# Who rounds the prepared weight sums in stage 2: ScalarE or VectorE

## The reference

```
h = relu(layernorm(x))
h_neigh = segment_sum(h[src], dst)
h = h @ Ws1 + h_neigh @ Wn1 + b1
h_neigh = segment_sum(h[src], dst)
out = x + h @ Ws2 + h_neigh @ Wn2 + b2
```

## Time and profile before

| what | value |
|---|---|
| median of three runs | 656.73 us |
| the profiled execution | 655.63 us |
| its span | 653.8 us |
| TensorE busy | 640.9 us (98%) |
| GpSimd busy | 210.3 us (32%) |
| VectorE busy | 286.0 us (44%) |
| ScalarE busy | 174.3 us (27%) |

### The profile page before, as it was taken

The page is one execution under the profiler, slowest core; times in us unless marked ns, Lnnn a source line. Parts: engine busy times, 40 slices in busy tenths (PEclk is TensorE's granted clock), DMA queues, the critical chain, the costliest instruction groups (busy, mean ns, idle before and its releaser), DMA issues.

```text
span 653.8 us, 8550 instructions
## 1 busy us (share of the span) xinstructions
PE 640.9 (98%) x3304; PEld 556.3 (85%) x3304; DVE 286.0 (44%) x392; ACT 174.3 (27%) x292; POOL 210.3 (32%) x198
## 2 busy tenths in 40 slices
PE   7999989999999999999999999999999999999997
PEld 5788778887899989999999988888888888887885
DVE  6763898871112111210022483325387987611111
ACT  5454243222123222313233122211334333100000
POOL 6224352000256666576580158003214012000000
PEclk9999999999999999999999999999999999999999
DMA  8622321003165676466754686444322242011111
GB/s 299 213 53 43 94 90 49 33 34 128 57 216 201 209 237 246 143 227 239 257 224 163 230 259 218 154 145 155 126 82 81 72 157 95 32 65 49 61 48 63
DMA packets 62726, 90.63 MB, mean 139 GB/s; under 512 B 16546, under 2 KB 34988, under 8 KB 62679
## 3 DMA queue, kind: packets, MB, share of 16 engines
q1 hardware_dynamic: 42342, 76.08, 34.6%
q10 hardware_dynamic: 20336, 13.91, 6.8%
HBM read 58.49 MB, written 31.48 MB: 138 GB/s over the span
## 4 chain that ended last, share of the span: by engine, by line
PE 62%; DMA 1%; DVE 0%; issue 0%; ACT 0%; POOL 0%; SPq 0%; DVEq 0%
PE PS L1274 29%; PE PS L1290 14%; PE PS L1237 10%; PE PS L1245 9%; DMA quarters<-ws_in 1%; DVE W_st L1021 0%; POOL prep_sum L624 0%; ACT W_st L750 0%; DVE s L1089 0%; ACT prep L801 0%; SPq L493 0%; DVEq L1088 0%
## 5 line engine op out<-in xcount | busy, mean ns | idle before, releaser
L1274 PE MATMUL PS<-right,left 128*128 128x512 f32 x840 | 190.6, 389 | 0.0
L1274 PEld LDWEIGHTS PS<-right,left 128*128 128x128 f32 x840 | 157.7, 188 | 32.7
L1109 PE MATMUL PS<-W,HT 128*128 128x512 f32 (+1 forms) x456 | 114.7, 399 | 2.7 <-ACT y_out L674 1.8
L1237 PE MATMUL PS<-HT,W_st 128*128 128x416 f32 (+1 forms) x576 | 110.7, 352 | 2.4 <-DVE W_st L1021 1.4
L1237 PEld LDWEIGHTS PS<-HT,W_st 128*128 128x128 f32 x576 | 107.9, 188 | 4.4 <-issue 3.4
L1109 PEld LDWEIGHTS PS<-W,HT 128*128 128x128 f32 (+1 forms) x456 | 81.3, 185 | 21.3 <-ACT y_out L674 2.9
L1245 PE MATMUL PS<-AT,y_st 128*128 128x416 f32 (+2 forms) x480 | 92.2, 351 | 0.0
L1245 PEld LDWEIGHTS PS<-AT,y_st 128*128 128x128 f32 (+1 forms) x480 | 90.1, 188 | 0.8
L657 POOL TENSOR_TENSOR left_sum<-h1T 128x640 f32<-128x640 f32 x24 | 41.9, 1747 | 150.2 <-PE PS L1274 119.9
L624 POOL TENSOR_TENSOR prep_sum<-quarters 128x512 f32<-128x512 f32 x40 | 52.7, 1320 | 100.0 <-PE PS L1109 62.8
L1290 PE MATMUL PS<-y_high,AT 128*128 128x512 f32 (+1 forms) x200 | 78.3, 392 | 0.0
(11 more groups left out here) (96 smaller groups left out, 476.9 us busy)
## 6 DMA issues: line engine op xcount, KB each, us to landing
sums_dram<-prep SPq DMA_DIRECT2D x40, 512.0 KB, 2.9
right<-sums_dram SPq DMA_DIRECT2D x40, 512.0 KB, 3.5
y_dram<-y_out ACTq DMA_DIRECT2D x18, 256.0 KB, 2.0
y_st_raw<-y_dram ACTq DMA_DIRECT2D x8, 576.0 KB
s<-x_in SPq DMA_DIRECT2D x18, 256.0 KB
out<-s SPq DMA_DIRECT2D x18, 256.0 KB
xin<-x_in SPq DMA_DIRECT2D x8, 512.0 KB, 11.6
W_raw<-wn_in SPq DMA_DIRECT2D x16, 256.0 KB, 5.1
```

The lines of the kernel that those rows point to most:

```text
L1109: ins = nc.tensor.matmul(PS[:r, bank, :], HT[:, a, k, t * P:t * P + r], W[:, k, b, :], start=first and m == 0, stop=last and m == 2)
L1237: ins = nc.tensor.matmul(PS[:, banks[c], 0:w_], W_st[:, a, k, :], HT[:, b, k, o_:o_ + w_], start=k == 0 and m == 0, stop=False)
L1274: ins = nc.tensor.matmul(PS[:, BANKS2[g % 8], :], left[:, k, a, i * P:(i + 1) * P], right[:, KB - 1 - k, b, :], start=k == 0 and j == 0, s ...
```

## The change

`prepare_high` moves from ScalarE's program to VectorE's, as a `tensor_copy` (a cast) in place of an activation with Copy. VectorE takes part 2j behind the LO part of `W_st` of tile j, and part 2j+1 behind the LO part of `y_st` of tile j. Part 1 is now behind tile 0's `y_st`, part 2 behind tile 1's `W_st`, and part 13 behind tile 6's `y_st`.

```diff
@@ ScalarE @@
-            def prepare_high(part):
-                for i in prepared(part):
-                    act.wait_ge(prep_summed, i + 1)
-                    nc.scalar.activation(prep[:, i % PREP, HI, :], prep_sum[:, i % PREP, LO, :], ACT.Copy).then_inc(prep_hi, 1)
-
             for j in range(KF - 1):
                 load_w_st(j + 1)
-                prepare_high(2 * j + 1)
                 w_st_high(j + 1)
                 load_y_st(j + 1)
                 h1_save(j, j % 2)
                 y_st_high(j + 1)
-                prepare_high(2 * j + 2)
@@ VectorE @@
+            def prepare_high(part):
+                for i in prepared(part):
+                    dve.wait_ge(prep_summed, i + 1)
+                    nc.vector.tensor_copy(prep[:, i % PREP, HI, :], prep_sum[:, i % PREP, LO, :]).then_inc(prep_hi, 1)
+
             for j in range(KF):
                 dve.wait_ge(wst_hi, j + 1)
                 nc.vector.tensor_tensor(W_st[:, LO, :, :], W_st_raw[:, LO, :, :], W_st[:, HI, :, :].bitcast(F32),
                                         ALU.subtract).then_inc(wst_lo, 1)
+                prepare_high(2 * j)
                 dve.wait_ge(yst_hi, 2 * j + 2)
...
+                prepare_high(2 * j + 1)
```

## The result

| | median us | range us | runs |
|---|---|---|---|
| before | 655.16 | 652.37 to 659.24 | 22 |
| changed | 652.43 | 650.46 to 656.15 | 21 |

The ratio is 0.9956 with a 95% interval of 0.994 to 0.9972: 1.8 to 3.9 us faster, 2.7 by the medians. The profiled execution of the changed kernel took 654.48 us, its span is 652.7.

What follows compares the result with a forecast made beforehand. TensorE, busy 98% of the span, was taken as the bound. Stall -1.5, casts 0 and `y_st` 0.1 made -1.4, so 654.2 us; with the runs' median 1.1 higher, 655.3, taken as 655.1. Range 653.8 to 657.5.

Steps and rivals of the forecast that it cites:

- the likeliest case: Whole kernel: the stage 2 stall goes and the casts hide behind TensorE; 655.1 us, own range 653.9 to 655.9, chance 0.57.
- The sum: Whole kernel: -1.5 for the stall, 0 for casts, 0.1 for `y_st`, so -1.4; 654.2 us, then taken as 655.1.
- the anchor: Whole kernel: the runs' median lies 1.1 us above the profiled execution's 655.63, which lifts 654.2 to 655.3; 655.1 taken.
- the gain: Stage 2: removing TensorE's 1.4 us wait, with slow first matmuls behind it, saves 1.5 us.
- The third rival: Runs' spread: all of it came from the wait for `W_st`, giving 653.9 us; held within the forecast's lower end, no separate chance.
- The removed part: ScalarE in stage 2: without high parts in its order, `W_st`'s high part starts when its load lands; the 1.4 us stall goes.
- The load of W: Stage 2, third tile: `W_st`'s load, issued at 230.03, lands after 4.5 us, leaving a margin of 3.4 to 4.4 us.
- The cast and its port: VectorE: 40 casts take turns with GpSimd on whole instructions, 0.28 us of turn each, bounds 0.28 and 1.46.
- GpSimd's batch: GpSimd: five sums, five low parts, the wait for quarters and shared turns take 19.6 to 22.0 us, typically 20.8; limit 21.9.
- the 2.6 us head start: First high part: VectorE is free at 178.1 where ScalarE began at 180.71, so sum 5 begins at about 191.
- The limit's place, cast 30: VectorE, ahead of tile 5's `y_st` low part: cast 30 must be done by about 303.3; second rival, 660.5 us, chance 0.14.
- `y_st`: Stage 2: its low part's margin thins from 1.5 to 0.2 us; costed at 0, bound 0.5 in each of three tiles.

Runs made afterwards that it cites:

- the odd parts alone: Against the kernel before, only the odd parts' high-part casts go to VectorE, the even parts stay on ScalarE behind `y_st`'s high part: ratio 0.999 (0.9965 to 1.0016).

## Why the prediction was wrong

The measured 652.46 us lies under the range of 653.8 to 657.5. The direction and the stall that goes were those of the likeliest case; the size was not.

- **The sum.** This is the step that failed, in two terms. First the anchor, the larger: I added 1.1 to the profiled execution's 655.63 to come to the median of three runs, 656.73. Over 22 runs the median is 655.16, so the term is -0.5; that is 1.6 of the 2.6 us between 655.1 and 652.46. Without it the sum gave 654.2, and I set that aside. Second the gain: I forecast 1.6 and held that even a perfect change takes no more than 1.4 to 1.7 us out of stage 2. The timed runs gave 2.7, at least 1.8. The profiles gave 1.6, the size I forecast but not made as I said: the waits are 0.8 of it, in place of 1.4, and the matmuls' step, which I did not see in the rows, is in the rest. Where the other 1.1 us of the timed gain come from stays open. The third rival, 653.9, came nearest by its number, not by its reason: it laid all of the runs' spread to this wait, and the changed kernel's runs still spread over 5.7 us, where those of before spread over 6.9.
- **Slips of sums.** 656.7 - 3 is 653.7 and not 653.9, 656.7 + 4 is 660.7 and not 660.5, and 1.4 us over 655.1 is 656.5 and not 656.2. None of them brings the measured time into the range.
- **The removed part.** The stall went, 26.58 to 25.04 us, though not from every execution (0.7 and 0.4 us in two of six profiles). But the reason I gave, that ScalarE's queue is cleared, is only one of two that suffice. In the changed kernel the same sum stands ahead of W on VectorE. It does no harm since it comes 4.7 us sooner, and the odd parts alone, which clear ScalarE's queue, gain nothing (0.999). I had both facts, the queue and the 2.6 us head start, and used the second only for the deadlines.
- **The load of W.** Costed at 4.5 us to landing, margin 3.4 to 4.4; it was 6.3 in the third tile, margin 2.3. The sooner quarters now go out just ahead of W's load there, a meeting that I had looked for at `y_st` only.
- **The cast and its port.** Right in kind: whole instructions take turns. 0.41 us alone, 1.5 beside GpSimd; it costs GpSimd 0.18, less than the 0.28 taken. The Trainium skill (SBUF — State Buffer, Who interferes with whom) says that the one that comes second fully blocks, and the trace agrees: 1.49 us for a cast of 0.41.
- **GpSimd's batch.** Predicted 20.8 us; from the loads of quarters at 185.55 and, six batches on, at 311.09 it is 20.9. Part of this is luck, as two errors cancel: the ten operations with all turns took 14.9 where I had 15.5, the wait for quarters 5.8 where I had 5.3. Sum 39 was to begin near 327 and began at 327.7. The limit's place, cast 30, is where TensorE did wait with two more casts each; that GpSimd is the bound there was not borne out (21.5 us a batch, and 21.9 wanted).
- **`y_st`.** No wait of TensorE, as forecast. The second tile's low parts ended at 199.67 for 205.2; its load, at 191.75, no longer ran right behind quarters, which had gone out at 185.55. In one of the six profiles of the changed kernel the weights waited 0.4 us for it.

## What to carry to other kernels

A wait for slow work from another stage costs by what stands behind it in the engine's order, so there are two cures: put the urgent work ahead, or make the slow work come sooner. They don't add up; joined without care they were 1% slower, since putting the urgent work ahead also held back what releases the next slow load. And a limit read from one profiled execution bounds that execution, not the median; nor is a stall found in one the mean stall, which here was 0.97 us and not 1.4. For gains of a few tenths of a per cent take several profiles of the kernel before, and anchor on more than three runs.

## What was not expected of the hardware

The same 132 matmuls and their weight loads, at granted clock 1.00 and without a gap, took 24.66 us in some tiles and 25.03 in others: 198.01 against 200.50 us over stage 2 in the two rows shown. The step can hold for many tiles. It changed at waits and also without one, and both kernels ran at either. What sets it is not known. At 1.2% of stage 2, 2.5 us, it is as large as the effect studied.
